# A convolution in split float32: the finished image is copied out of PSUM by ScalarE, and a DMA in SBUF adds the middle products

## The reference, cut to what matters

```python
k = masks                                    # 12 log-polar bins of a 9x9 window, each an average
xp = log_pooling(x)                          # x: (32, 256, 28, 28) f32
out = conv(xp, w_conv1, stride=(4, 3)) + conv(x, w_center) + b_center
mean, var = out.mean((0, 2, 3)), out.var((0, 2, 3))
out = (out - mean) * rsqrt(var + 1e-5) * gamma + beta
return relu(out + x)
```

## Time and profile before

| | |
|---|---|
| median of 3 runs (lowest, highest) | 1656.84 us (1656.44, 1657.08) |
| the profiled execution: its own time, its span | 1657.47 us, 1655.8 us |
| PE busy | 1483.6 us (90%) |
| DVE busy | 1419.4 us (86%) |
| ACT busy | 641.7 us (39%) |
| mean granted TensorE clock | 0.949 |

### The profile page before, as it was taken

The page is one execution under the profiler, slowest core; times in us unless marked ns, Lnnn a source line. Parts: engine busy times, 40 slices in busy tenths (PEclk is TensorE's granted clock), DMA queues, the critical chain, the costliest instruction groups (busy, mean ns, idle before and its releaser), DMA issues.

```text
span 1655.8 us, 22787 instructions
## 1 busy us (share of the span) xinstructions
PE 1483.6 (90%) x8468; PEld 1481.7 (89%) x8468; DVE 1419.4 (86%) x1327; ACT 641.7 (39%) x689; POOL 112.5 (7%) x146
## 2 busy tenths in 40 slices
PE   6999999999999999999999999999999999992000
PEld 6999999999999999999999999999999999992000
DVE  7999898988988889898898888988989988886323
ACT  3234434334334343433433434343343333434423
POOL 1000000000000000000000000000000000000000
PEclk8999999999999999999999999999999999997555
DMA  6455554555545555455545555545554555579999
GB/s 198 105 130 144 134 133 123 124 143 123 118 123 131 143 134 134 125 121 143 132 111 121 131 142 134 135 126 120 141 130 115 120 132 141 134 244 420 425 425 382
DMA packets 65479, 268.75 MB, mean 162 GB/s; under 512 B 7616, under 2 KB 7616, under 8 KB 65472
## 3 DMA queue, kind: packets, MB, share of 16 engines
q1 hardware_dynamic: 42176, 173.38, 31.1%
q0 software_dynamic: 18432, 69.61, 24.3%
q10 hardware_dynamic: 4864, 25.69, 3.7%
HBM read 218.07 MB, written 50.58 MB: 162 GB/s over the span
## 4 chain that ended last, share of the span: by engine, by line
PE 86%; SPq 5%; DMA 4%; DVE 3%; ACT 1%; issue 1%; ACTq 0%; DVEq 0%; POOLq 0%
PE acc L664 29%; PE acc L665 29%; PE acc L666 29%; SPq L311 3%; DMA phase<-x 2%; SPq L308 2%; DMA row<-x_wide 1%; DMA out<-phase 1%; DVE pooled L448 1%; ACT phase L440 0%; DVE pooled_split L449 0%; DVE inner_split L449 0%; ACT m_copy L396 0%; DVE y_stage L448 0%; DVE row3v L448 0%
## 5 line engine op out<-in xcount | busy, mean ns | idle before, releaser
L380 ACT ACTIVATE pooled_split<-pooled 128x1456 fp32r<-128x1456 f32 x192 | 273.4, 1425 | 611.0 <-DVE pooled L448 611.0
L449 DVE TENSOR_TENSOR pooled_split<-pooled,pooled_split 128x1456 fp32r<-128x1456 f32 x192 | 315.2, 1669 | 0.3 <-ACT pooled_split L380 0.3
L664 PE MATMUL acc<-pooled_split,w_first 128*128 128x364 f32 x768 | 253.3, 330 | 3.9 <-DVE pooled_split L449 3.9
L665 PE MATMUL acc<-pooled_split,w_first 128*128 128x364 f32 x768 | 253.8, 330 | 0.0
L666 PE MATMUL acc<-pooled_split,w_first 128*128 128x364 f32 x768 | 252.9, 329 | 0.0
L665 PE MATMUL acc<-pooled_split,w_outer 128*128 128x364 f32 x768 | 252.2, 328 | 0.0
L664 PE MATMUL acc<-pooled_split,w_outer 128*128 128x364 f32 x768 | 252.2, 328 | 0.0
L666 PE MATMUL acc<-pooled_split,w_outer 128*128 128x364 f32 x768 | 251.8, 328 | 0.0
L664 PE MATMUL acc<-inner_split,w_first 128*128 128x406 f32 (+1 forms) x640 | 223.5, 349 | 13.5 <-DVE inner_split L449 10.1
L666 PE MATMUL acc<-inner_split,w_first 128*128 128x406 f32 (+1 forms) x640 | 223.1, 349 | 0.0
L665 PE MATMUL acc<-inner_split,w_first 128*128 128x406 f32 (+1 forms) x640 | 223.0, 348 | 0.0
(11 more groups left out here) (81 smaller groups left out, 2139.4 us busy)
## 6 DMA issues: line engine op xcount, KB each, us to landing
row<-x_wide SPq DMA_DIRECT2D x64, 558.0 KB, 3.7
row<-x_wide POOLq DMA_DIRECT2D x64, 558.0 KB, 7.3
ends<-x_wide SPq DMA_DIRECT2D x64, 504.0 KB, 3.9
ends<-x_wide POOLq DMA_DIRECT2D x64, 504.0 KB, 5.8
x_pad<-x SPq DMA_DIRECT2D x64, 392.0 KB, 3.1
y_dram<-y_stage SPq DMA_DIRECT2D x31, 784.0 KB, 8.7
phase<-y_dram SPq DMA_DIRECT2D x30, 784.0 KB, 28.6
phase<-x SPq DMA_DIRECT2D x30, 784.0 KB, 30.3
```

The costliest lines, as they stand in the source:

```text
L380: nc.scalar.activation(view(pooled_split, 2 * j * PAIR, (1, PAIR)), view(pooled, (PAIRS * c + j) % 2 * PAIR, (1, PAIR)), ACT.Copy)\
L449: sub = lambda out_, a, b: nc.vector.tensor_tensor(out_, a, b, ALU.subtract)
L664: nc.tensor.matmul(place, hi_w, hi_in, start=start, stop=False)
L665: nc.tensor.matmul(place, lo_w, hi_in, start=False, stop=False)
```

## The change

The last step of an image is done in another way. ACT copies banks 0 to 3 into `y_stage` (`copy_y`, between pairs 1 and 2 of the next image's `c` = 0). ACT and DVE put the middle sums in a buffer of their own, `middle_sums` (also the place for unused output of `measure`). POOL, in `c` = 1 between its two other accumulating DMAs, adds `middle_sums` onto `y_stage` with one accumulating DMA inside SBUF, 784 KB; its landing is the new `y_ready`. PE waits for the two ACT copies (`y_copied`). The save by SP and both `measure` calls move from `c` = 0 (and early `c` = 1) into `c` = 1, behind the new `y_ready`; the pivot moves there too. The last image is finished on DVE as before. `image_steps(LAST)` of SP therefore issues the save of image 30 in the last half of the last image.

```diff
             def image_sums(image, first=False):
                 for c in range(CH):
                     s = CH * image + c
                     wait_first(row2_begun, 16 * (s + 1))
                     add_from(image, c, row2, -1, W + 3).then_inc(row2_ready, 16)
+                    if c == 1 and not first:
+                        wait_first(middle_taken, image + FREE)
+                        wait_first(y_copied, CH * image + FREE)
+                        pool.dma_start(y_stage[:, :], middle_sums[:, :], accum_op=ALU.add).then_inc(y_ready, 16)
                     wait_first(ends_begun, 16 * (s + 1))
                     add_from(image, c, ends, 2, W).then_inc(ends_ready, 16)
...
-                    if c == 0 and not first:
-                        sp.wait_ge(y_ready, CH * image + FREE)
+                    if c == 1 and not first:
+                        sp.wait_ge(y_ready, 16 * image)
                         sp.dma_start(y_dram[bass.ds(image - 1, 1)].rearrange("n p f -> p (n f)"),
                                      y_stage[:, :]).then_inc(y_saved, 16)
...
             def copy_m1(image):
                 act.wait_ge(m_done, image + 1)
+                wait_from_one(act, y_ready, 16 * image)
                 wait_from_one(act, y_measured, MOMENTS * image)
-                nc.scalar.activation(view(m1_copy, 0, (HALF, CH), (H, U), (1, H)),
+                nc.scalar.activation(view(middle_sums, H, (HW, CH), (2 * H, U), (1, H)),
                                      view(acc, MBANK * BANK, (BANK, CH), (PITCH, U), (1, H)), ACT.Copy)\
                     .then_inc(m1_copied, 1)
 
+            def copy_y(image):
+
+                act.wait_ge(pooled_done, PAIRS * CH * (image + 1))
+                wait_from_one(act, y_saved, 16 * image)
+                wait_from_one(act, y_measured, MOMENTS * image)
+                for o in range(CH):
+                    nc.scalar.activation(view(y_stage, o * HW, (H, 2), (2 * H, U), (1, H)),
+                                         view(acc, 2 * o * BANK, (BANK, 2), (H, U), (1, H)), ACT.Copy)\
+                        .then_inc(y_copied, 1)
...
-                    if c == 1 and not first:
-                        measure(image - 1, 1)
...
                     for j in range(PAIRS):
+                        if c == 0 and j == 2 and not first:
+                            copy_y(image - 1)
                         split_pooled(s, c, j)
-                    if c == 0 and not first:
-                        measure(image - 1, 0)
+                        if c == 1 and j < CH and not first:
+                            measure(image - 1, j)
...
+                    if second and c == 1:
+                        make_pivot()
                     dve.wait_ge(row3v_ready, s + 1)
...
                     lo_of_pooled(s, c, 0)
-                    if c == 0 and not first:
-                        take_y(image - 1)
                     dve.wait_ge(ends_ready, 16 * (s + 1))
...
-                            pe.wait_ge(y_ready, CH * image + FREE)
+                            pe.wait_ge(y_copied, CH * image + FREE)
```

More of the change, by code:

```diff
@@ L105, in conv_bn_relu_program @@
         y_stage = sb("y_stage", CH * HW)
-        m1_copy = sb("m1_copy", CH * HALF)
+        middle_sums = sb("middle_sums", CH * HW)
         D1, D2, VD, SD = 0, MIDDLE, 2 * MIDDLE, 2 * MIDDLE + 2 * HALF
@@ L195, in conv_bn_relu_program @@
         middle_taken = sem("middle_taken")
+        y_copied = sem("y_copied")
         y_ready = sem("y_ready")
         y_saved = sem("y_saved")
+        last_y_ready = sem("last_y_ready")
         pivot_ready = sem("pivot_ready")
@@ L250, in wait_first, with image_sums @@
                 nc.gpsimd.sem_inc(sum_turns, 1)
-            def image_sums(image):
+            def image_sums(image, first=False):
                 for c in range(CH):
@@ L256, in image_sums @@
                     add_from(image, c, row2, -1, W + 3).then_inc(row2_ready, 16)
+                    if c == 1 and not first:
+                        wait_first(middle_taken, image + FREE)
+                        wait_first(y_copied, CH * image + FREE)
+                        pool.dma_start(y_stage[:, :], middle_sums[:, :], accum_op=ALU.add).then_inc(y_ready, 16)
                     wait_first(ends_begun, 16 * (s + 1))
                     add_from(image, c, ends, 2, W).then_inc(ends_ready, 16)
-            image_sums(0)
+            image_sums(0, first=True)
             with pool.Fori(1, IMAGES) as image:
@@ L385, in copy_m1 @@
                 act.wait_ge(m_done, image + 1)
+                wait_from_one(act, y_ready, 16 * image)
                 wait_from_one(act, y_measured, MOMENTS * image)
-                nc.scalar.activation(view(m1_copy, 0, (HALF, CH), (H, U), (1, H)),
+                nc.scalar.activation(view(middle_sums, H, (HW, CH), (2 * H, U), (1, H)),
                                      view(acc, MBANK * BANK, (BANK, CH), (PITCH, U), (1, H)), ACT.Copy)\
                     .then_inc(m1_copied, 1)
+            def copy_y(image):
[6 more added lines that the diff above has]
+                        .then_inc(y_copied, 1)
             def measure(image, o):
-                act.wait_ge(y_ready, CH * image + o + 1 + FREE)
+                if image is LAST:
+                    act.wait_ge(last_y_ready, o + 1)
+                else:
+                    act.wait_ge(y_ready, 16 * (image + 1))
                 act.wait_ge(pivot_ready, 1)
@@ L395, in measure @@
                     wait_from_one(act, y_measured, MOMENTS * image + KINDS * o + kind)
-                    nc.scalar.activation(m1_copy[:, :], view(y_stage, o * HW, (1, HW)), function,
+                    nc.scalar.activation(view(middle_sums, 0, (1, HW)), view(y_stage, o * HW, (1, HW)), function,
                                          bias=minus_pivot[:, o:o + 1],
@@ L498, in take_middle, with take_last_y @@
                 dve.wait_ge(m1_copied, image + 1)
-                wait_from_one(dve, y_saved, 16 * image)
-                wait_from_one(dve, y_measured, MOMENTS * image)
                 m2 = view(acc, (MBANK + CH) * BANK, (BANK, CH), (PITCH, U), (1, H))
[L502 to L508, removed]
+                m1 = view(middle_sums, H, (HW, CH), (2 * H, U), (1, H))
+                add(view(middle_sums, 0, (HW, CH), (2 * H, U), (1, H)), m2, m1)
+                sub(view(middle_sums, H, (HW, CH), (2 * H, U), (1, H)), m1, m2).then_inc(middle_taken, 1)
+            def take_last_y():
+                dve.wait_ge(pooled_done, PAIRS * CH * IMAGES)
+                dve.wait_ge(middle_taken, IMAGES + FREE)
+                dve.wait_ge(y_saved, 16 * LAST)
+                dve.wait_ge(y_measured, MOMENTS * LAST)
                 for o in range(CH):
-                    y = view(y_stage, o * HW, (H, 2), (2 * H, U), (1, H))
-                    add(y, view(acc, 2 * o * BANK, (BANK, 2), (H, U), (1, H)), y).then_inc(y_ready, 1)
+                    columns = (H, 2), (2 * H, U), (1, H)
+                    add(view(y_stage, o * HW, *columns), view(acc, 2 * o * BANK, (BANK, 2), (H, U), (1, H)),
+                        view(middle_sums, o * HW, *columns)).then_inc(last_y_ready, 1)
             def make_pivot():
-                dve.wait_ge(y_ready, CH + FREE)
+                dve.wait_ge(y_ready, 16)
                 for o in range(CH):
@@ L610, in image_steps @@
                     lo_of_pooled(s, c, 2)
-                    if second and c == 0:
-                        make_pivot()
-            dve.sem_inc(y_ready, FREE)
+            dve.sem_inc(y_copied, FREE)
             dve.sem_inc(middle_taken, FREE)
@@ L622, in _ @@
             take_middle(LAST)
-            take_y(LAST)
+            take_last_y()
             dve.wait_ge(y_measured, MOMENTS * IMAGES)
```

## The result

| | before | changed |
|---|---|---|
| median (lowest to highest), 21 runs each | 1656.48 us (1655.33 to 1658.13) | 1659.27 us (1658.40 to 1660.79) |
| ratio, 95% interval | | 1.0016 (1.0010 to 1.0023) |
| span of the profiled execution | 1655.8 | 1658.5 |

The change costs 2.8 us, 0.17%: less than the 3.7 forecast, and just inside the bound of 0.2% that I had set for no change. The interval leaves out 1, so a small loss is real.

What follows compares the result with a forecast made beforehand. The prediction took PE to bound the kernel up to about 1470 us and DMA from there to the end. Startup -0.4 and hinge +4.1 summed to +3.7 us, a median of 1660.5 us, range 1656.8 to 1667.0.

Steps and rivals of the forecast that it cites:

- ACT's queue in half 1: In the loop, measure delays ACT's splits; DVE idles 0.1 then 2.1 us per image, covered by its earlier 1.94 us idle.
- Startup: At image 1, ACT's copies let PE go at 81.0 instead of 81.38: 0.4 us gained, lower clock still following.
- The addition's landing: Last image's half 1: row2 issued at 1460.57 lands at 1467.4, the addition 3.9 us later, at 1471.3.
- Rival B: Addition at the plain transfer rate, 2.4 instead of 3.9 us: +2.2, 1659.0 us; sign: loads start before 1476.0; chance 0.22.
- The save: Save of image 30, issued at 1471.4, takes 5.0 us (bounds 4.3 and 8.8) and lands at 1476.4, when loads start.
- one us for one us: End of phase 1: every us by which the loads start later or earlier moves the end by one us.
- the hinge: Passage from PE-bound phase 1 to DMA-bound phase 2, where first loads start 6.1 us later; cost 4.1 us.
- the filled hole: From 1480 to 1483 the DMA ran below its rate before; a backlog fills that, giving back 0.8 us.
- C: At the hinge, the addition takes 7.8 us or the save its 8.8 again: +7.6 to +11, 1664.4 to 1668; chance 0.16.
- D: In the loop, a cover is thinner than read and PE waits; 1 us per image gives 1690; chance 0.05.
- E: At image 1, the shorter gap leaves the clock unlowered, saving 2.6 us: +1.1, 1657.9 us; chance 0.06.
- F: PE's wait at image 1 vanishes with its low clock, the hinge costs only 2.6: -3.4, 1653.4 us; chance 0.05.

Runs made afterwards that it cites:

- gate_box4: Kernel before, with SP's loads of the first four places also waiting for box4 of the last half; 1659.75 us, ratio 1.0017.
- release_both: Changed kernel, first four places' loads issued ahead of the save of image 30, which nothing awaits until phase 2's second round; 1659.32 us, ratio 1.0017.
- gate_pooled: Kernel before, with SP's loads of the first four places also waiting for the last half's first pooled sum; 1661.97 us, ratio 1.0031.
- early_before: Kernel before, with the loads of the first four places moved into the last image's half 0; 1656.43 us, ratio 0.9998.
- add_first: Changed kernel, with the addition issued ahead of row2's accumulate in POOL's list for half 1; 1659.47 us, ratio 1.0017.

## Why the prediction was right, point by point

- **PE bound in the loop, no gain from DVE's relief: right.** PE 200.00 of 200 us after; the 49 us of DVE came back as waits.
- **The copies come as early as DVE's additions: right.** Done at 721.66 + 1.52 = 723.2, forecast 723.8; a copy takes 0.76 of a pair, not 0.83. PE wants the banks at 727.15, 4 us later.
- **ACT's queue in half 1: right.** DVE waits 1.7 us per image for split 2, forecast 2.1. It was covered as said: the low part comes at 710.33, which is 0.37 earlier, with PE.
- **Startup: -0.4 forecast, -0.37 measured.** The lower clock after the gap stayed in this execution (0.66 from 80 to 90 us in both traces).
- **The addition's landing: 1471.3 forecast, 1470.1 measured** (1460.72 plus 9.4), 1470.5 in the time of the kernel before, which is 0.37 behind. The price from two accumulates in a row was good: `row2` landed at 1466.3 and the addition 3.8 us later, forecast 3.9. The 0.8 us come from `row2`, which was issued 0.2 us earlier than forecast and landed after 6.3 instead of 6.8. Rival B, the plain rate with 2.4 us, is out by this, although the sign that I gave for it, loads before 1476.0, occurred, and its 1659.0 us is nearer to the measured 1659.27 than my 1660.5. The sign was too coarse, as other terms move the loads too, and the nearness is luck.
- **The save: 5.0 forecast, 4.4 measured,** near the lower bound of 4.3. So the loads came at 1474.54, or 1474.91 in the time of before, instead of 1476.4, 1.5 us early, of which 0.6 come from the save and the rest from the earlier landing of the addition. The start of the loads is the term that was mis-sized. By my own rule of one us for one us it should have made the hinge 2.6 instead of 4.1 us; it cost 3.1. The other 0.5 us is in how the loads get under way, which short windows of the changed kernel show:

```profile
1475.00:1475.50 0.50, 0.50 (x5) 0.50 (x5) 0.50 (x2) 0.00 (x0) 0.00 (x0) 1.00 0.05 13
1475.50:1476.00 0.50, 0.50 (x5) 0.50 (x5) 0.50 (x1) 0.00 (x0) 0.00 (x0) 1.00 0.78 125
1476.00:1476.50 0.50, 0.50 (x5) 0.50 (x5) 0.50 (x1) 0.00 (x0) 0.00 (x0) 1.00 0.72 238
1476.50:1477.00 0.50, 0.50 (x5) 0.50 (x4) 0.50 (x2) 0.00 (x0) 0.00 (x0) 1.00 0.95 389
1477.00:1480.00 3.00, 3.00 (x19) 3.00 (x19) 3.00 (x3) 2.81 (x4) 0.00 (x0) 1.00 1.00 414
```

My sum let 425 GB/s flow from 1.2 us after the issue. They flow from 1.0 us after it, but at 125 and 238 GB/s for the first microsecond. Redone with these rows, 13, 125, 238 and 389 GB/s for half a us each and 414 for 2.63 us until 1479.63 (1480 less 0.37) bring 1.47 MB where 3.10 came before: 1.63 MB, 3.8 us, less the filled hole of 0.8 us, is 3.0. Measured: 3.07.
- **What the loss is made of: half right.** I priced it as the late start of the first loads, and a late start alone does cost that (gate_box4). But with the start put back nearly to its old place (release_both) the loss stayed, because the traffic that I had priced only as part of the delay then stood in the full stretch. In the changed kernel itself the DMA's idle time did not grow (5.3 us against 5.4), its work did, by 3.2 us. The number came out, as both descriptions count the same bytes missing at 1480; that it did not need the right one of the two is luck.
- **Slower or within 0.2%:** I gave 0.50 and 0.45. It came out at 0.17% (ratio 1.0016), within, so on the side that I held slightly less likely.
- **Rivals.** C and D did not occur; E and F neither in this execution, though E's clock was seen elsewhere (next section).

## What to carry to other kernels

Where a kernel ends in a stretch in which the DMA is full, traffic added to that stretch costs about its own time, whoever waits for it: here 3.1 us for an addition of 3.4, and 1.9 for one of 2.3. Moving traffic out of it into idle DMA time gives that back, but only down to the next bound: the same move was worth 2.8 us to the changed kernel and nothing to the kernel before. An engine that waits for another engine in steady state gives nothing back when it is relieved, but it may in the first rounds, before the pipeline has filled; there look for idle time that comes back one round later. Before shortening a chain of transfers, look whether the stretch it goes through is full.

## What the runs showed of the hardware that I had not expected

**The clock.** PE's idle time at image 1 was not always followed by the lower clock. PE's timeline in gate_box4, whose instructions up to there are those of the kernel before, and the windows from 80 to 90 us of gate_box4 and of before:

```profile
81.43 0.45 PE L665 MATMUL acc<-inner_split,w_first 128*128 128x392 f32 x1 [3.35 <-DVE y_stage L449]
81.72 0.34 PE L666 MATMUL acc<-inner_split,w_first 128*128 128x392 f32 x1
```

```profile
80.00:90.00 10.00, 8.57 (x49) 8.57 (x50) 9.79 (x15) 2.09 (x2) 1.73 (x2) 1.00 0.71 181
```

```profile
80.00:90.00 10.00, 8.62 (x34) 8.62 (x35) 9.79 (x15) 2.14 (x2) 0.86 (x1) 0.66 0.72 184
```

The idle time is the same, 3.35 and 3.36 us, but here PE stays at 2.4 GHz, with 49 matmuls in the 10 us instead of 34, and SP's last `row2` comes 2.1 us earlier (1453.97 against 1456.06). The clock of that stretch was 1.00 in gate_pooled and release_both too, 0.83 in early_before and add_first, 0.66 in before and changed. So two profiled executions can differ by 2 us for this alone, nearly as much as the effect under study. That it also makes the spread of the times (1655.33 to 1658.13 of before) is argued, not shown.

**Accumulating DMAs.** One that reads and writes SBUF stays far from the rate of a plain transfer: 784 KB took 3.4 us of all 16 engines, 236 GB/s, where the other accumulates have 173 and the plain queue 337 by the same reckoning. The Trainium skill, in "DMA: Bandwidth & Descriptors", section "Anatomy of one DMA", has a transfer from POOL cost about 2.0 us plus its bytes over 436 GB/s. As an estimate from that page, the addition alone would land 3.8 us after its issue; here it landed 9.3 to 10.2 us after it, behind a `row2` of 558 KB, which by the same formula accounts for 1.3 us more, and 8.0 us after it in add_first, where it stood ahead of `row2`. The measurement decides.
